# Transformer block with cross-attention and a routed feed-forward layer: order of transfers and conversions at the seams between stages

## What is computed

```python
# attention: 16 query heads of 96 in 4 groups, 4 key/value heads, keys over context and x together
hidden = concatenate([context, latents], axis=1)
q, k, v = latents @ Wq.T, hidden @ Wk.T, hidden @ Wv.T
attn = softmax(einsum('bkgqd,bksd->bkgqs', q, k) / sqrt(96))
out = einsum('bkgqs,bksd->bkgqd', attn, v) ... @ Wo.T
# feed-forward layer
rw = sum(top_k(h @ gate_w, 2))
shared = relu(h @ up_w) ** 2 @ down_w
routed = ((h @ fc1_w) @ expert_w * rw) @ fc2_w
return layernorm(shared + routed, gamma, beta)
# block
x = x + attention(layernorm(x), ctx)
x = x + ffn(layernorm(x), ...)
```

## Time and profile before

| | us |
|---|---|
| median of 3 runs (2229.25 to 2234.17) | 2231.41 |
| the profiled execution | 2228.66 |
| its span, first to last instruction | 2226.9 |
| PE busy in it (9948 matmuls) | 2163.1 (97%) |
| DVE, ACT, POOL busy | 772.4, 655.6, 698.9 |
| mean share of the full TensorE clock that was granted | 0.993 |
| DMA, mean rate | 117 GB/s |

### The profile page before, as it was taken

How to read it: one execution, slowest core, us unless ns; L and a number is a source line. 1 busy time by engine, 2 the same in 40 slices (tenths; PEclk the granted TensorE clock), 3 DMA queues, 4 the chain that set the end, 5 groups by cost and what they waited for, 6 DMA issues and landing times.

```text
span 2226.9 us, 30285 instructions
## 1 busy us (share of the span) xinstructions
PE 2163.1 (97%) x9948; PEld 1779.9 (80%) x9948; DVE 772.4 (35%) x1340; ACT 655.6 (29%) x1121; POOL 698.9 (31%) x566
## 2 busy tenths in 40 slices
PE   6999999999999999999999999999999999999997
PEld 6788888887777777777888778888887788888885
DVE  4223222166666666650110222222211142222222
ACT  3011111146666666561111222212123321111110
POOL 3500000136666666663212424100004422222221
PEclk9999999999999999999999999999999999999998
DMA  5632322625555555433443525312214532222221
GB/s 162 216 123 107 129 85 86 178 67 142 129 137 140 128 138 140 114 100 109 150 136 107 179 93 176 127 61 75 94 58 134 172 105 86 88 96 93 88 90 41
DMA packets 228028, 260.45 MB, mean 117 GB/s; under 512 B 73584, under 2 KB 141424, under 8 KB 227824
## 3 DMA queue, kind: packets, MB, share of 16 engines
q1 hardware_dynamic: 172224, 179.01, 25.4%
q10 hardware_dynamic: 55728, 80.48, 12.7%
HBM read 167.28 MB, written 91.88 MB: 116 GB/s over the span
## 4 chain that ended last, share of the span: by engine, by line
PE 75%; issue 13%; POOL 5%; DVE 3%; DMA 3%; ACT 1%; ACTq 1%; SPq 0%; POOLq 0%; DVEq 0%
PE psum L116 23%; PE psum L117 23%; PE psum L118 23%; POOL operands L1605 3%; PE psum L788 3%; PE psum L184 1%; DMA operands<-h_scratch 1%; DVE operands L960 1%; DVE small L939 0%; DMA staging<-in_ctx 0%; ACT psum L866 0%; POOL operands L1044 0%; ACTq L368 0%; PE psum L1406 0%; PE psum L1405 0%
## 5 line engine op out<-in xcount | busy, mean ns | idle before, releaser
L116 PE MATMUL psum<-operands 128*128 128x512 f32 (+2 forms) x3016 | 1181.5, 392 | 39.3 <-DVE operands L298 15.1
L117 PE MATMUL psum<-operands 128*128 128x512 f32 (+2 forms) x3016 | 1164.7, 386 | 0.0
L118 PE MATMUL psum<-operands 128*128 128x512 f32 (+2 forms) x3016 | 1162.5, 385 | 0.0
L116 PEld LDWEIGHTS psum<-operands 128*128 128x128 f32 x3016 | 570.1, 189 | 156.4 <-issue 17.4
L118 PEld LDWEIGHTS psum<-operands 128*128 128x128 f32 x3016 | 569.9, 189 | 112.5
L117 PEld LDWEIGHTS psum<-operands 128*128 128x128 f32 x3016 | 571.6, 190 | 97.2
L721 POOL TENSOR_TENSOR operands<-staging,operands 128x512 fp32r<-128x512 f32 x192 | 247.5, 1292 | 189.1 <-ACT operands L875 189.1
L939 DVE TENSOR_REDUCE small<-psum 128x1 f32<-128x576 f32 x256 | 193.4, 756 | 152.3 <-PE psum L788 152.3
L1044 POOL TENSOR_TENSOR operands<-staging,operands 128x512 fp32r<-128x512 f32 x94 | 121.1, 1299 | 387.8 <-ACT operands L1039 387.5
L1605 POOL TENSOR_TENSOR operands<-operands 128x640 fp32r<-128x640 f32 x64 | 100.4, 1573 | 320.7 <-ACT operands L1600 320.4
L1486 DVE TENSOR_TENSOR staging<-staging 128x512 f32<-128x512 f32 x64 | 46.3, 744 | 308.7 <-ACT staging L1452 307.9
(11 more groups left out here) (84 smaller groups left out, 1036.2 us busy)
## 6 DMA issues: line engine op xcount, KB each, us to landing
h_scratch<-staging ACTq DMA_DIRECT2D x80, 256.0 KB, 2.1
operands<-h_scratch SPq DMA_DIRECT2D x64, 320.0 KB, 3.1
operands<-recip_scratch SPq DMA_DIRECT2D x64, 192.0 KB, 3.0
o_scratch<-staging SPq DMA_DIRECT2D x64, 192.0 KB, 3.3
operands<-o_scratch SPq DMA_DIRECT2D x64, 192.0 KB, 2.6
operands<-q_hi_scratch ACTq DMA_DIRECT2D x14, 768.0 KB, 6.1
operands<-q_lo_scratch ACTq DMA_DIRECT2D x14, 768.0 KB, 6.5
staging<-in_wqkv SPq DMA_DIRECT2D x36, 256.0 KB, 3.3
```

What stands on the lines that cost most here:

```text
L116: e.matmul(o, lh, rh, start=first, stop=False)
L117: e.matmul(o, lh, rl, start=False, stop=False)
L118: return e.matmul(o, ll, rh, start=False, stop=last)
```

## The change

- p0: ACT issues the x load of batch 0 behind the highs of the first three ctx halves instead of ahead of them; half 12 (a V half) gets its low from POOL instead of DVE; the transposes of batch 0 come later in the V product and use three banks, 5, 6 and 7, so that transpose k waits for the low of chunk k - 3.
- p0 to A: SP loads halves 16 to 31 of the Q weights (before: 16 to 23) ahead of the x load of batch 1 and of the first store; the other eight stay between the stores.
- B to C: the highs and lows of tile 0's units move ahead, from head 2G - 2 to head G + 1 (the lows of units 2 and 3 to head 2G - 1); SP issues the loads of tile 1's units 0, 1 and 2 earlier between the last heads' transfers; POOL makes the lows of tile 1's units 0 and 1 ahead of the last scale.
- C, last batch: jobs go between units 1 and 2 of the next tile on SP, ACT and POOL, instead of behind the units; ACT issues the x1 load instead of SP; the last tile uses banks 4 and 5, and stage D waits for its addition at group 1 only.
- D to E: the job of the first chunk of the routed part (FC) moves from stage D's last table to the head of `JOBS_E`, which has six jobs then.
- E, last tile: first half of the shared part, routed part, second half.

The diff, cut to its core (counts of ranges that follow from it are left out):

```diff
-        def norm_z(tag, xn, last_free):
+        def norm_z(tag, xn, last_free, first=(6, 7)):
...
-                e.wait_ge(*past(zl, b * DK + k - 1))
+                e.wait_ge(*past(zl, b * DK + k + 1 - len(banks(b))))
...
-        BY_DVE, BY_POOL = [0, 1, 2, 3, 4, 5, 12, 13, 14, 15], [6, 7, 8, 9, 10, 11]
+        BY_DVE, BY_POOL = [0, 1, 2, 3, 4, 5, 13, 14, 15], [6, 7, 8, 9, 10, 11, 12]
...
         def p0_sp(e):
-            for n in range(NF + 8):
+            for n in range(NF + 16):
                 raw_load(e, n)
...
-            at = {(0, 0): [0, 1], (0, 1): [2], (0, 4): [3], (0, 7): [4], (1, 2): [5], (1, 4): [6], (1, 6): [7]}
+            at = {(0, 4): [0, 1, 2], (0, 5): [3], (0, 6): [4], (0, 7): [5], (1, 0): [6], (1, 1): [7]}
...
+            for n in range(3):
+                raw_high(e, n)
             a_load(e, x_r, 0)
-            for n in range(10):
+            for n in range(3, 10):
                 raw_high(e, n)
...
-            "a", XN, lambda e, b: e.wait_ge(*past(a_acc, b * A_EV)))
+            "a", XN, lambda e, b: e.wait_ge(*past(a_acc, b * A_EV)), (5, 6, 7))
...
-            more = list(range(NF + 8, NF + 2 * QC))
+            more = list(range(NF + 16, NF + 2 * QC))
...
             put_recip(NI - 1, 2 * G - 2)
+            c_load_unit(e, 0, 1, 0)
             spread(NI - 1, 2 * G - 2)
+            put_recip(NI - 1, 2 * G - 1)
             store(NI - 1, 2 * G - 4)
-            c_load_unit(e, 0, 1, 0)
-            put_recip(NI - 1, 2 * G - 1)
+            c_load_unit(e, 0, 1, 1)
             spread(NI - 1, 2 * G - 1)
-            c_load_unit(e, 0, 1, 1)
             store(NI - 1, 2 * G - 3)
             store(NI - 1, 2 * G - 2)
+            c_load_unit(e, 0, 1, 2)
             store(NI - 1, 2 * G - 1)
...
-                    if last and hh == 2 * G - 2:
-                        c_units_lo(e, 0)
+                    if last and hh == G + 1:
+                        c_units_lo(e, 0, (0, 1))
+                    if last and hh == 2 * G - 1:
+                        c_units_lo(e, 0, (2, 3))
...
-            for o in range(2 * G - 4, 2 * G):
+            for o in range(2 * G - 4, 2 * G - 1):
                 scale(NI - 1, o)
+            c_units_lo(e, 1, (0, 1))
+            scale(NI - 1, 2 * G - 1)
...
-                    if last and hh == 2 * G - 2:
+                    if last and hh == G + 1:
                         c_units_hi(e, 0)
...
-                     5: [("e", 12), ("e", 13), ("e", FC)]}
-        JOBS_E = [("e", c) for c in (14, 15, *range(FC + 1, FC + LC))]
+                     5: [("e", 12), ("e", 13)]}
+        JOBS_E = [("e", c) for c in (FC, 14, 15, *range(FC + 1, FC + LC))]
...
-                    for u in range(0 if n != 1 else 2, 4):
+                    for u in range(0 if n != 1 else 3, 4):
+                        if u == 2:
+                            for j in (jobs or {}).get(t - 1, []):
+                                job_load(e, j, m)
+                                m += 1
                         c_load_unit(e, b, t, u)
...
-                    for j in (jobs or {}).get(t, []):
-                        job_load(e, j, m)
-                        m += 1
-                    if jobs and t == 0:
-                        d_load(e, x1_d, 0)
...
                     if n:
-                        c_units_hi(e, n)
+                        c_units_hi(e, n, (0, 1))
+                    for j in (jobs or {}).get(t - 1, []):
+                        job_hi(e, j, m)
+                        m += 1
+                    if n:
+                        c_units_hi(e, n, (2, 3))
...
+                    if jobs and t == 0:
+                        e.wait_ge(*past(cc_st, ST * 16))
+                        d_load(e, x1_d, 0)
...
+        def c_bank0(n):
+            return 4 if n == B * ST - 1 else 2 * (n % 2)
...
                         e.wait_ge(*past(d_ev, b * ND + (D_CUM[g - 2] if g >= 2 else 0)))
+                        if g == 1:
+                            e.wait_ge(*past(cc_x1, B * ST))
...
-            e.wait_ge(*past(cc_x1, B * ST))
+            e.wait_ge(*past(cc_x1, B * ST - 1))
...
             job(1)
+            job(2)
             e_load(e, 0, 1, 0)
-            job(2)
+            job(3)
             e_load(e, 0, 1, 1)
-            job(3)
             job(4)
+            job(5)
             e_load(e, 0, 1, 2)
...
-            e.wait_ge(*past(e_lo, n * 4 + 4))
-            for h in range(2):
-                for k in range(FC, NK):
-                    m = step(ST - 1, k, h)
-            m.then_inc(e_half, 1)
             for h in range(2):
                 for k in range(FC):
+                    if h == 0 and k % EU == 0:
+                        e.wait_ge(*past(e_lo, n * 4 + k // EU + 1))
                     m = step(ST - 1, k, h)
                 m.then_inc(e_half, 1)
+                if h == 0:
+                    for hf in range(2):
+                        for k in range(FC, NK):
+                            m = step(ST - 1, k, hf)
+                    m.then_inc(e_half, 1)
```

56 lines of the change are left out of this document (29 added, 27 removed).

## The result

The changed kernel takes **2207.76 us** in the median of four runs (2205.26 to 2209.24), the kernel before 2231.24 on the same chip (2229.25 to 2234.17): ratio 0.9893, 95% interval 0.9875 to 0.9910. The forecast was 2206.3 in a range of 2198 to 2216. The profiled execution has a span of 2203.5 us against 2226.9. PE executes 9948 matmuls as before, in 2157.3 us instead of 2163.1.

A forecast was written before the change was run, and what follows sets the result against it. PE bounds the kernel nearly everywhere, so only seams can win: 1.2 + 0 + 11.3 + 3.4 + 1.5 + 7.7 = 25.1 us off 2228.66 gives 2203.6, or 2206.3 as median; range 2198 to 2216.

The forecast's parts named there:

- Head: Batch 0's z: stage's end moves from 42.18 to about 41.0 with the clock's loss; gain 1.2 us.
- x lands when DVE becomes free, so its place costs the norm nothing: Head: x lands at 15 against DVE's start on it at 14.93 before, so z is ready at the same time, 27.8.
- Ring: Q weight loads ahead of stores: 5.3 us removed, but batch 1's x load holds the first store, costing 5.3; gain 0.
- Attention to projection: Attention's end to output projection: waits of 3.60 and 2.86 us and half clock behind them go; gain 11.3 us.
- Projection to FFN: Unit waits of 2.1 us go, and banks 4 and 5 save 1.28 us; gain 3.4 us.
- x1 moves off SP's queue: Projection to FFN: without the 2 MB x1 load ahead on SP, unit loads land in 7.0 us, not 10.0.
- FFN to the last stage: Start wait of 4.46 us goes, but the six-job chain makes PE stand about 4 us later; gain 1.5 us.
- the start of the chain: Last stage: first job's lows at about 1774.6, five more at 4.45 us each, ending at 1796.9.
- 0.7 for half clock behind that chunk: Last stage's first tile: some 0.7 us net of clock lost behind the wait at the last chunk.
- Last tile: Last stage's last tile: 5.66 us wait for the fourth unit and half clock go; PE ends at 2208.7; gain 7.7 us.
- gaps of 2.8 us or more: PE at seams: a stretch at half clock, 1.2 instead of 2.4 GHz, shows after each gap this long.

The follow-up runs named there:

- e4: Changed kernel with only batch 0's x load put back ahead of the first ctx highs; 2207.71 us, stage A starts at 39.60 instead of 41.44.
- e10: Changed kernel with only the banks and table of batch 0's transposes put back (two banks); 2213.28 us, stage A starts at 44.84.
- e1: Changed kernel with batch 1's x load issued behind the first pair of stores instead of ahead of it; 2203.5 us, ratio 0.9860.
- e8: Changed kernel with only SP's loads of tile 1's units put back behind the spreads and stores at attention's end; 2213.19 us, ratio 0.9905.
- e11: Changed kernel with only the highs and lows of tile 0's units put back behind the last head's lows; 2214.04 us, ratio 0.9913.
- e7: Changed kernel with only the 2 MB x1 load put back from ACT's queue to SP's; 2209.48 us, ratio 0.9883.
- e6: Changed kernel with only the last stage's start put back: FC's job in stage D's last table, five jobs behind; 2208.73 us, ratio 0.9885.
- e5: Changed kernel with the six last jobs over three pairs of half buffers instead of one, and FC's highs early; 2201.64 us, ratio 0.9861.
- e9: Changed kernel with e4, e1 and e5 together; 2195.71 us, ratio 0.9831, span 2194.1.

## Why the prediction was right, and where its steps were off

- **Head: 1.2 forecast, 0.74 measured** (0.7 to 1.7 over the nine executions with this head, against the one trace of before). The sum came near for wrong reasons, so that it did is luck. PE started at 11.98 and not at 9.4 (in the other executions 9.6 to 11.5), x landed at 16.49 and not at 15, and z was ready at 29.98, not 27.8. The step that failed is "x lands when DVE becomes free, so its place costs the norm nothing": e4 shows a cost of 1.8 us (0.9 to 2.0 over the executions). The banks, taken as a way to soften that, are the part that wins (e10, 3.4). That the moved low of half 12 costs nothing failed too; the last section has its price.
- **Ring: 0 forecast.** Measured was a gap of 4.29 us and 1.7 by the clock, 6.0 against the old 5.3, so 0.7 lost (0.4 by the instants, 0.4 to 3.0 over the nine executions with this ring; the half clock was taken at 1.7, as in the changed kernel's trace, and most of the others had more). Mechanism and landing time were right: e1 takes away only the order on the queue and wins 5.2.
- **Attention to projection: 11.3 forecast, 11.3 measured** (from -0.19 to 11.10). e8 and e11 find both causes. That this came out to a tenth is luck in part: undone one by one they give 8.9, and what the half clock takes differs between executions.
- **Projection to FFN: 3.4 forecast, 4.1 measured** (11.10 to 15.21). The gaps of 1.60 and 0.49 us near 1248 and 1265 and the 1.28 of the earlier trace rows are gone. But the reason given, that x1 moves off SP's queue, is refuted by e7. The traces tell the rest apart by place, though no run undoes it: from tile 1's addition to the last tile's the changed kernel won 2.6 us, where the jobs moved, and from there to stage D's first matmul 1.5, where the banks did.
- **FFN to the last stage: 1.5 forecast, 0.3 measured** (e6, within what executions differ by; 0.5 between the two traces, from 15.21 to 15.73). The kind of wait was as forecast, and its pace, 4.5 us a job; PE stood 3.88 us against 4. What was off is when the chain ends. DVE's lows of the first job and the last low, in the changed kernel:

```profile
1758.31 2.51 DVE L1056 TENSOR_TENSOR operands<-staging,operands 128x512 fp32r<-128x512 f32 x2 [4.28 <-ACT operands L1051]
...
1782.55 0.69 DVE L1056 TENSOR_TENSOR operands<-staging,operands 128x512 fp32r<-128x512 f32 x1 [1.56 <-ACT operands L1051]
```

With the 15.21 us that this trace is ahead, the first job was done at 1776.0 on the scale of before and not at 1774.6, and PE took the last chunk (1783.35) at 1798.6 and not at 1796.9; before, it was 1799.1. So the mis-sized term is the start of the chain, 1.4 us, and with some 0.2 more on the way 1.7 of the 2.2 us were not won. The other term, 0.7 for half clock behind that chunk, was nothing here: from the last chunk to the second addition it took 30.06 us, 30.04 before. The clock was low while PE was ahead of the chain, where a slower PE only waits less. In e7 it was low behind the last chunk (taken at 1786.90), and the same stretch took 31.8. So a gain of 0.5 is also what a favourable execution gives. e5 took out what was left.
- **Last tile: 7.7 forecast, 7.67 measured** (15.72 to 23.39); this part was not undone by itself, but from tile 14's addition to PE's end the changed kernel and all twelve edits of it took 26.0 us, and the kernel before 33.7. The working by matmuls (45 before the fourth unit is wanted, 5.5 us of delay) needed no unknown price.

The forecast sum was 25.1, the spans differ by 23.4. By the instants the head is 0.5 short, the ring 0.4, the last stage 1.0; attention lost 0.5 in this execution, within what executions differ by; and the projection's seam gave 0.7 more.

## What to carry to other kernels

When a step is moved past a queue, look for the large transfer that moves with it: a 2 MB load is cheap where nothing is issued behind or beside it for the 7.6 to 12.8 us that it took in these runs, and dear ahead of a store that a two-place staging waits for. A chain of load, high, low over one pair of buffers passes on every delay, and here half of a head start (6.4 us at the first link, 3.1 at the last); three pairs, with the order that they allow, broke it where the earlier start alone did not. And before a transfer is put later to let others pass, find who waits for it: here the norm of batch 0 did, the matmuls let ahead of it had time to spare.

## What the runs showed of the hardware

**Work moved to POOL slowed DVE beside it.** DVE's and POOL's rows of the changed kernel's head:

```profile
23.71 1.14 DVE L174 TENSOR_SCALAR small<-small 128x4 f32<-128x4 f32 x1
...
26.21 1.60 DVE L178 TENSOR_SCALAR staging<-staging,small 128x1024 f32<-128x1024 f32 x1 [0.15 <-DVE small L175]
```

```profile
23.54 3.72 POOL L304 TENSOR_TENSOR operands<-staging,operands 128x512 fp32r<-128x512 f32 x3 [2.78 <-ACT operands L299]
```

Operations on 128x4 elements that take 0.16 us elsewhere in this norm took 1.14 and 1.07, and the first of four equal 128x1024 ones took 1.60 instead of 0.80. The third POOL low is the one that the change moved: before, POOL had two there, and the four together took 2.98 us instead of 3.77. The two small ones took 1.15 and 1.10 in the kernel before, too. So each of these POOL lows cost the norm 0.8 to 1.0 us. Not every DVE operation is slowed: the statistics (L164, 16.63 to 21.47) took 4.84 us beside three other POOL lows (from 16.98, 3.78 us), and the same eight in batch 1's norm (at 100.86), with no POOL instruction beside them, took 4.83. The Trainium skill (SBUF — State Buffer, "SBUF: two separate sides") says that GpSimd shares a port pair with a DVE operation in a 2-port mode or with two SBUF inputs, as an exclusive lock that the first to start holds for its whole instruction while the other blocks. The trace agrees in the size of each delay, somewhat under one POOL low of 1.27 us, and in that some DVE operations go on beside POOL; which mode each of them uses no trace here shows. Half 12's low was not put back to DVE by itself.

**The clock fell behind shorter gaps than I had taken.** I wrote of gaps of 2.8 us or more. e9's stretch of 15 us around its gap of 2.04 us shows PEclk 0.89, and e7's ten us around a gap of 1.87 us in attention 0.83; behind e8's gap of 2.20 us, and behind one of 2.02 us in attention in e4 (586 to 596), it stayed at 1.00:

```profile
85.00:100.00 15.00, 12.96 (x51) 10.20 (x50) 4.94 (x8) 2.99 (x5) 8.85 (x10) 0.89 0.72 246
```

```profile
588.00:598.00 10.00, 8.13 (x32) 6.21 (x31) 5.19 (x10) 4.82 (x10) 3.36 (x3) 0.83 0.27 71
```

```profile
1024.00:1034.00 10.00, 7.80 (x35) 6.13 (x34) 0.00 (x0) 1.16 (x3) 1.97 (x2) 1.00 0.62 203
```

So a gap of about 2 us is worth 2 to 4, and which of them is not settled by its length.
